# Cross-attention and mixture-of-experts block on Trainium2: the weighing of each score group moved to the group's end, its jobs between second and third score

## The reference

```
x = x + cross_attention(layernorm(x), ctx, ctx, mask)      # first block
x = x + ffn_block(layernorm(x))                            # second block

cross_attention: q = x @ w_q.T, k = ctx @ w_k.T, v = ctx @ w_v.T   # 16 heads of 16
    q, k = rope(q), rope(k)
    scores = where(mask == 0, -10000, q k^T / 4)           # 512 x 1024 per head and batch
    return (softmax(scores) @ v) @ w_o.T
ffn_block: layernorm, causal self attention over 256 positions, 4 KV heads, layernorm,
    router with top 2 of 8 experts, gelu experts, weighted sum
```

## Time and profile before

| | |
|---|---|
| median of 3 runs | 791.83 us (788.49 to 794.24) |
| the profiled execution | 785.16 us, its span 783.4 us |
| PE busy | 694.3 us (89%) |
| DVE busy | 557.6 us (71%) |
| ACT busy | 493.5 us (63%) |
| POOL busy | 354.6 us (45%) |
| mean granted TensorE clock | 0.948 |

### The profile page before, as it was taken

One profiled execution on the slowest core, in us unless ns is written; L12 is line 12 of the kernel. 1 busy time (PEld: TensorE's weight loads), 2 busy tenths in 40 slices (PEclk: granted clock), 3 DMA queues, 4 the chain that ended last, 5 costly groups with the idle time before them and its releaser, 6 DMA issues. The chain is left out here.

```text
span 783.4 us, 13504 instructions
## 1 busy us (share of the span) xinstructions
PE 694.3 (89%) x4402; PEld 424.7 (54%) x4402; DVE 557.6 (71%) x919; ACT 493.5 (63%) x980; POOL 354.6 (45%) x262
## 2 busy tenths in 40 slices
PE   2355799999999999999999999879978879999996
PEld 1252344444444443444333433557767768889985
DVE  4968778778888778887889893367985435555553
ACT  1110567788777788777777778566645057667673
POOL 4867435129440359068658920000055703544444
PEclk9775789999999999999999999999989899999999
DMA  9476257665868473338858820089437456533321
GB/s 264 164 249 184 113 178 245 208 165 192 272 205 238 121 231 114 116 147 282 282 202 291 272 112 2 1 294 421 108 84 251 156 119 139 96 36 36 39 28 20
DMA packets 59719, 130.73 MB, mean 167 GB/s; under 512 B 8868, under 2 KB 26308, under 8 KB 58196
## 3 DMA queue, kind: packets, MB, share of 16 engines
q1 hardware_dynamic: 33364, 72.86, 28.2%
q0 software_dynamic: 16848, 35.95, 17.9%
q10 hardware_dynamic: 9440, 21.06, 9.0%
HBM read 80.80 MB, written 69.39 MB: 192 GB/s over the span
## 5 line engine op out<-in xcount | busy, mean ns | idle before, releaser
L756 DVE TENSOR_REDUCE mx<-wide 128x2 f32<-128x1024 f32 x256 | 307.3, 1222 | 69.3 <-PE wide L910 68.1
L618 ACT ACTIVATE probs<-narrow 128x512 f32<-128x512 f32 x492 | 265.4, 599 | 73.5 <-PE narrow L949 72.3
L910 PE MATMUL wide<-kst,qst 49*128 49x512 f32 x512 | 177.2, 475 | 14.7 <-DMA kst<-k_pieces 7.8
L949 PE MATMUL narrow<-qst,kst 51*128 51x512 f32 x492 | 186.2, 451 | 2.5 <-ACT probs L618 2.2
L949 PEld LDWEIGHTS narrow<-qst,kst 51*128 51x128 f32 x492 | 79.0, 185 | 133.8 <-issue 49.6
L964 PE MATMUL values<-probs,vaug 128*17 128x512 f32 x1024 | 135.3, 600 | 1.4 <-ACT probs L618 0.8
L1714 POOL DMA_INDIRECT out<-res,token x39 | 60.7, 1557 | 94.4 <-DMA out<-res,token 60.5
L910 PEld LDWEIGHTS wide<-kst,qst 49*128 49x128 f32 x512 | 71.4, 194 | 29.4 <-DVE mx L756 16.9
L1246 POOL DMA_DIRECT2D out<-xt x4 | 5.5, 1378 | 113.8 <-DVE xt L1441 113.8
L1739 ACT ACTIVATE h_hi<-narrow 128x512 fp32r<-128x512 f32 x39 | 23.3, 599 | 42.5 <-PE narrow L1819 42.5
L455 POOL TENSOR_TENSOR turn_b<-turn_a,tab 128x1024 f32<-128x1024 f32 x10 | 24.0, 2401 | 55.6 <-ACT turn_a L612 55.1
(11 more groups left out here) (289 smaller groups left out, 1350.3 us busy)
## 6 DMA issues: line engine op xcount, KB each, us to landing
list_rows<-in_w ACTq DMA_DIRECT2D x56, 342.0 KB, 5.4
kst<-k_pieces SPq DMA_DIRECT2D x14, 784.0 KB
k_pieces<-turn_a SPq DMA_DIRECT2D x16, 512.0 KB, 4.3
w_hi<-w_hi SPq DMA_DIRECT2D x16, 512.0 KB, 11.0
w_lo<-w_lo SPq DMA_DIRECT2D x16, 512.0 KB, 11.9
turn_a<-in_w POOLq DMA_DIRECT2D x11, 512.0 KB, 5.3
w_hi<-turn_b POOLq DMA_DIRECT2D x11, 512.0 KB, 3.0
w_lo<-turn_a POOLq DMA_DIRECT2D x11, 512.0 KB, 4.5
```

Of the source, the lines that this page charges most:

```text
L618: nc.scalar.activation(probs[:, n % NP, :], score_bank(n), ACT.Exp, scale=DK ** -0.5).then_inc(exp_done, 1)
L756: last = nc.vector.tensor_reduce(mx[quad % 2][:, qt, :, hp, kh], slot[:, :, :], axis=AX.X, op=ALU.max)
L910: last = nc.tensor.matmul(slot[:, i, :], qst[u % 3][r:r + R_MAX, h, P * qt:P * qt + P], kst[u % 3][r:r + R_MAX, h, 512 * kh:512 * kh + 512 ...
L949: nc.tensor.matmul(score_bank(n), kst[u % 3][r:r + R_ALL, h, P * kt:P * kt + P], qst[u % 3][r:r + R_ALL, h, :], start=True, stop=True).the ...
```

## The change

Three things move, and no instruction is added or removed:

- In a group, the jobs other than the maxima, `nm` and `mxt` go between the second and the third score (they were at the end); weigh(g - 1) goes to the end of group g (it was between the second and the third score).
- The copy to `outT` moves from group 8q + 8 to group 8q + 9, behind the exponential of the second score. The job `out` moves from time 8q + 9.1 to 8q + 10.1, so by one group, for all quads but the last two.
- `oT` moves from g + 2.2 to g + 3.2, so by one group.

```
-            timed += [(g + 2.2, ("oT", b - 1))] + ...
+            timed += [(g + 3.2, ("oT", b - 1))] + ...
     for quad in range(QUADS - 1):
-        timed.append((8 * quad + 9.1, ("out", quad)))
+        timed.append((8 * quad + (10.1 if quad < QUADS - 2 else 9.1), ("out", quad)))
...
-        steps = [("score", 4 * g)] + [("job", j) for j in tops[:1]] + [("score", 4 * g + 1)] + [("weigh", g - 1)] * (g > 0)
+        inner = [j for j in rest if j[0] not in ("nm", "mxt")]
+        steps = [("score", 4 * g)] + [("job", j) for j in tops[:1]] + [("score", 4 * g + 1)] + [("job", j) for j in inner]
         steps += [("score", 4 * g + 2)] + [("job", j) for j in tops[1:2]] + [("score", 4 * g + 3)]
-        return steps + [("job", j) for j in tops[2:] + rest]
+        return steps + [("job", j) for j in tops[2:] + rest if j not in inner] + [("weigh", g - 1)] * (g > 0)
...
         for g, now in enumerate(group_steps):
             if g in FILL_AT:
                 fill(FILL_AT.index(g))
+            summed = g // 8 - 1 if g > 8 and g % 8 == 1 else None
             for what, j in now:
                 if what == "score":
                     exponential(j)
-                elif what == "weigh" and j % 8 == 7:
-                    take_out(j // 8)
                 elif what == "job" and j[0] == "pair":
                     exponential_of_pair(g)
                 elif what == "job":
                     job(j)
+                if summed is not None and (what, j) in (("score", 4 * g + 1), ("job", ("pair", g))):
+                    take_out(summed)
```

More of the change, by code:

```diff
@@ L67, in attention_order @@
         if b > 0:
-            timed += [(g + 2.2, ("oT", b - 1))] + [(g + x, ("oP", b - 1, n // 2, n % 2)) for n, x in enumerate((8, 10, 11, 12))]
+            timed += [(g + 3.2, ("oT", b - 1))] + [(g + x, ("oP", b - 1, n // 2, n % 2)) for n, x in enumerate((8, 10, 11, 12))]
     for quad in range(QUADS - 1):
-        timed.append((8 * quad + 9.1, ("out", quad)))
+        timed.append((8 * quad + (10.1 if quad < QUADS - 2 else 9.1), ("out", quad)))
     timed += [(GROUPS - 12.8, ("oT0", B - 1)), (GROUPS - 9.5, ("oP0", B - 1))]
```

## The result

The changed kernel took 801.37 us (median of 4, 797.18 to 804.26) where the kernel before took 792.9 in the same comparison: a ratio of 1.0116 (1.0084 to 1.0148). Run again beside 29 runs of before it took 800.81, 1.0094 (1.0063 to 1.0126). Forecast was 793.3, within 1% of before, with a range up to 801; the time lies just above it.

What follows compares the result with a forecast made beforehand. The prediction took PE, busy 89% of the span, as the bound, with light groups held by ACT's exponentials. Its terms summed to +1.4 us, on the runs' median of 791.83 giving 793.3, with an 80% range of 785.5 to 801.

Steps and rivals of the forecast that it cites:

- Light groups: Groups of only scores and maxima: the weighing no longer waits for exponentials, 0.06 us less in each of 22, -1.2 us.
- mxt: Five groups with mxt, now ahead of the weighing: period 3.19 us instead of 3.09, +0.5 us in all.
- projections: Groups with a projection: PE is the bound, so their period stays at 3.23 us.
- The copy: The outT copy, third on ACT, holds the next weighing: 3.14 us instead of 2.75 in four groups, +1.5 us.
- pair group: Within groups 118 to 127, the last copy moves behind the pair's exponential: 0.5 us either way, counted as nothing.
- Jobs that meet: Groups 40 to 42 and their like take 10.13 us instead of 9.54, +1.8; groups 32 to 36 and like, +0.5.
- Casts beside POOL: DVE's L764 casts stretched by POOL: two tied to the rope lose some 0.5 us each, -1.0, bounds +2 and -4.5.
- Queues: Transfers behind q, k, v and the ropes, and SP's max rows, come no later against the scores: counted as nothing.
- Start-up: First groups, xn copies between ACT's second and third exponential: DVE's idle time filled sooner, -0.7 us (0 to -1.4).
- (a): Weighing was the brake: light periods fall to 2.3 us, 786.9 in all, chance 0.10; larger form 782, chance 0.04.
- (c): The outT copy throws ACT back and the delay passes to the next period: +11 us, 804, chance 0.13.
- (b): None of the block's fifteen DVE casts meets POOL, 789.8 us, or twice as many do, 797.8; chance 0.08.

Runs made afterwards that it cites:

- late copy: The kernel before with only the copy to outT half a group later, behind the fourth exponential of its group: 797.9 us, ratio 1.0067.
- turned, old start, no cast: Kernel before with jobs and weighing moved within groups from group 3 on, outT copy, out, oT unmoved, L764's cast a second reduction: 798.2 us, 1.0059.
- before with LEAD 4 later: The kernel before with maxima ending four groups ahead of their quad instead of three, for quads 2 to 15 alone: 778.9 us, 0.9951.

## Why the prediction was wrong

- **Light groups, mxt, projections:** right, 2.59, 3.19 and 3.22. (22 times 0.06 is 1.3, not 1.2.)
- **The copy:** the mechanism was right (the weighing waits for it behind ACT's third place, 3.20 for 3.14), the size too small. Forecast were 3.6 us (1.5 + 3 x 0.55 + 2 x 0.2); the medians give 5.7 in both orders, the rows 4.2 in the turned one. Missing were 0.9 in the pair group, "counted as nothing", and 0.06 in each light group, because the release takes somewhat longer behind the copy. The remaining 1.5 isn't traced to the copy; casts and clock are the candidates.
- **Jobs that meet:** right, 10.27 for 10.13 and 18.45 for 18.3 to 18.4. The prediction's own sum gave +0.1 to +0.2 over 18.22 and it took +0.25 without a reason; +0.23 came, by luck.
- **Casts beside POOL, -1.0:** right in that the rope's casts went; wrong in that I counted only those. Quads 3 and 7 now have casts of 1.5 us, quad 11 of 2.07, quad 14 of 1.83. By the periods long casts cost 4.5 us before and 2.9 in the changed kernel's first trace, so -1.6; in its second, with the subtraction stretched and one fall of the clock, some 4.4. A cast's price is also the fall of the clock behind it, 1.15 us, which I had not seen: in the trace of before no cast was followed by one.
- **Queues, counted as nothing, "no later":** this failed. The max rows were stored with more time in hand (5.4 us to the first score instead of some 4), but behind POOL's stores of w, and took 6.7 (7.1 in the second trace: 384.66 to 391.79). It cost 1.3 us (0.5).
- **Start-up, -0.7:** this is the step with the wrong sign, +2.1 in the trace and +3.7 (1.4 to 4.6 us by its interval, read on 792.9) when done alone. I argued that DVE's idle time is filled sooner. Shown instead are a wait of 2.1 us for ACT's xn copies where it had been 1.15, one of 2.2 us for DVE's xT_lo, and a second fall of the clock. Which of the three weighs most isn't separated.
- **Rivals:** (a) is refuted by 2.59; (c) by the periods behind a copy; of (b) neither form came: there are four casts of 1.5 us or more again.

The steps that failed are thus three terms: the start, taken as -0.7 and measured at +2.1, the transfers' queues and the last copy's pair group, both taken as nothing and measured at +1.3 and +0.9. The first block's sum was +1.4, of which -0.7 at the start: +2.1 elsewhere. The traces show +2.1 at the start and +3.9 to +5.0 elsewhere, 5.9 to 7.0 in all. Of the 5.6 us between 1.4 and 7.0, the three terms are 5.0; copies and meeting jobs add 0.7, the casts take 0.6 back, and some 0.5 stays open. The medians say 8.5. The rest is within what two executions of this kernel differ by (415.1 and 419.0 for the changed one's block).

## What to carry over

In a schedule where engines hand over every half microsecond, price not only the periods that repeat but the places that occur once: the start, the last groups, and the meetings with a slow background engine. Put a small copy where its engine pauses, not where its input happens to be long ready. A stall of some 1 to 2 us on PE can cost another 1.15 us through the clock, so look behind each stall for a stretch at 0.50. And when a parameter such as LEAD moves one thing, list what else the code derives from it (here the form of a whole group).

## Of the hardware

- PE's granted clock fell to 1.2 GHz behind waits of its weight loads of only 1.1 us (the kernel before run again, at 188.7), 1.4 us (late copy, at 191.2 and 300.4) and 2.2 us (turned, old start, no cast, at 390.0), and not every time: it stayed at 2.4 GHz behind waits of 1.78 and 2.11 us in the changed kernel (488.41, 387.72).
- A DVE copy or subtraction of 128x16 took up to 2.27 us instead of 0.18 beside a POOL operation of 2.4 us (before with LEAD 4 later, at 371.11; 1.67, 1.98 and 2.07 above); a reduction of the same data stayed at 0.19 in the 14 cases in which it ran beside one.
- Max rows of 8 KB took 6.7 to 7.1 us from issue to their first user, which waited for them, when POOL's two stores of 512 KB had left ahead of them, the second 0.6 to 0.8 us ahead; in the kernel before, ahead of such stores, they took 4.2 us once (405.79) and held up no score some 4 us later in another quad.
- The same stretch of the second block (last weighing to `y_first`) took 126.6 to 128.6 us in four traces and 138 to 141 in thirteen, the longer ones with 17 to 20 us at 1.2 GHz in the middle of it. The medians of whole sets of runs differ by the same 10 us. The cause wasn't looked for.
